# GNN kernel: the words of edge counts are written by ScalarE as 16-bit integers into their place, instead of through a float copy and GpSimd

## The reference

```python
def _ngcf_conv(x, W1, W2, src, dst, n_nodes):
    deg_out = clip(segment_sum(ones, src), 1.0); deg_in = clip(segment_sum(ones, dst), 1.0)
    norm = rsqrt(deg_out[src] * deg_in[dst])
    h_src, h_dst = x[src], x[dst]
    msg = (h_src @ W1 + h_src * h_dst @ W2) * norm[:, None]
    return x @ W1 + segment_sum(msg, dst, n_nodes)

h = maximum(layernorm(x), 0.0)
h = relu(conv(h, W1_1, W2_1)); h = conv(h, W1_2, W2_2)
return x + h
```

## Time and profile before

| | |
|---|---|
| median of the runs | 516.54 us |
| the profiled execution | 518.48 us, its span 516.8 us |
| busy, share of the span | PE 94%, PEld 88%, DVE 79%, ACT 49%, POOL 43% |
| granted TensorE clock, mean | 0.981 |
| chain that ended last | PE 72%, DVE 17%, issue 5%, ACT 2%, DMA 2%, POOL 1% |
| largest groups | `los` L663 136.3 us; `slab` L895 128.2; `hots` L1025 118.7; `words` L463 79.2; `saved` L1034 53.4 |

### The profile page before, as it was taken

The page is one execution under the profiler, slowest core; times in us unless marked ns, Lnnn a source line. Parts: engine busy times, 40 slices in busy tenths (PEclk is TensorE's granted clock), DMA queues, the critical chain, the costliest instruction groups (busy, mean ns, idle before and its releaser), DMA issues.

```text
span 516.8 us, 19829 instructions
## 1 busy us (share of the span) xinstructions
PE 485.1 (94%) x7949; PEld 455.4 (88%) x7949; DVE 410.2 (79%) x1040; ACT 252.4 (49%) x726; POOL 220.9 (43%) x425
## 2 busy tenths in 40 slices
PE   2699999989997997999999999999999999999995
PEld 2577788878786887999999999999999999999995
DVE  6978999999999986987777777776766666666662
ACT  0279999999998795433333333333111121112111
POOL 3336879788999483453333433333100001100000
PEclk9879999999999898999999999999999999999998
DMA  2257102020201000000000000000000110020011
GB/s 68 82 95 94 47 21 64 3 63 3 65 1 43 2 3 1 3 4 2 3 4 3 3 3 2 3 4 3 3 1 3 21 26 1 3 44 1 3 29 20
DMA packets 17912, 10.89 MB, mean 21 GB/s; under 512 B 14144, under 2 KB 16496, under 8 KB 17821
## 3 DMA queue, kind: packets, MB, share of 16 engines
q1 hardware_dynamic: 17117, 7.60, 7.7%
q0 software_dynamic: 672, 2.01, 1.4%
q10 hardware_dynamic: 32, 0.01, 0.0%
HBM read 6.21 MB, written 3.33 MB: 18 GB/s over the span
## 4 chain that ended last, share of the span: by engine, by line
PE 72%; DVE 17%; issue 5%; ACT 2%; DMA 2%; POOL 1%; SPq 0%; DVEq 0%; ACTq 0%; POOLq 0%
PE diff L988 34%; PE iota_bank L988 17%; DVE los L663 9%; PE slab L895 8%; PE diff L879 4%; PE diff L959 2%; PE diff L966 1%; DVE stats L671 1%; ACT hots L1025 1%; PE slab L937 1%; DMA los<-in_dst_dram 1%; PE diff L955 1%; PE turn_t L937 1%; DVE rows L652 1%; DVE late L704 1%
## 5 line engine op out<-in xcount | busy, mean ns | idle before, releaser
L663 DVE TENSOR_TENSOR los<-mixed,iota_bank 128x5120 bf16<-128x5120 bf16 x49 | 136.3, 2810 | 7.0 <-PE slab L895 6.9
L895 PEld LDWEIGHTS slab<-hots,los 128*128 128x128 bf16 x2352 | 122.0, 99 | 17.5 <-issue 4.4
L895 PE MATMUL slab<-hots,los 128*128 128x98 fp8e5 x2352 | 128.2, 211 | 3.0 <-DVE los L663 2.9
L551 POOL TENSOR_TENSOR work<-work,h 128x64 f32<-128x64 f32 x98 | 31.4, 321 | 214.7 <-DVE work L774 214.7
L1025 ACT ACTIVATE hots<-diff 128x784 f16<-128x784 f32 x147 | 118.7, 847 | 9.1 <-PE diff L879 8.8
L988 PE MATMUL diff<-late,mixed 128*128 128x128 f16 x1616 | 104.4, 219 | 0.0
L988 PEld LDWEIGHTS diff<-late,mixed 128*128 128x128 fp8e4 x1616 | 98.7, 99 | 0.4
L988 PE MATMUL diff<-los,mixed 128*128 128x129 f16 x1470 | 95.7, 220 | 0.0
L988 PEld LDWEIGHTS diff<-los,mixed 128*128 128x128 fp8e4 x1470 | 89.3, 98 | 0.3
L463 POOL TENSOR_SCALAR words<-saved 128x784 uint16<-128x784 uint16 x49 | 79.2, 1617 | 7.8 <-ACT saved L1034 7.4
L879 PE MATMUL diff<-select,mixed 80*128 80x392 f16 x294 | 69.4, 342 | 8.4 <-ACT hots L1025 5.0
(11 more groups left out here) (172 smaller groups left out, 537.8 us busy)
## 6 DMA issues: line engine op xcount, KB each, us to landing
x_sb<-in_x_dram SPq DMA_DIRECT2D x4, 384.0 KB
rows_table<-rows SPq DMA_DIRECT2D x6, 252.0 KB
mixed<-rows_table SPq DMA_DIRECT2D x18, 84.0 KB
out_dram<-x_sb SPq DMA_DIRECT2D x8, 128.0 KB
los<-in_dst_dram SPq DMA_DIRECT2D x1, 750.0 KB
out_dram<-x_sb SPq DMA_DIRECT2D x4, 80.0 KB
out_dram<-x_sb SPq DMA_DIRECT2D x4, 48.0 KB
rows_table<-rows SPq DMA_DIRECT2D x1, 180.0 KB
```

The source lines that it names most:

```text
L551: nc.gpsimd.tensor_tensor(out=pair[a][:, 1], in0=s_sum[a], in1=h[:, b], op=ALU.mult).then_inc(product_ready, 1)
L663: nc.vector.tensor_tensor(out=los[:, b % LOS_RING].rearrange("e s (v t) -> e s v t", t=2), in0=key, in1=val, op=ALU.is_equal).then_inc(los ...
L895: ins = nc.tensor.matmul(to, los[:, u // 2 % LOS_RING, u % 2 * ULOWS + low], pairs, start=(step == 0), stop=(step == USTEPS - 1), skip_gro ...
```

## The change

- `words` gets 18 slots (SLOTS) for each block and `v` instead of 16 words: slots 0 to 7 hold the first unit's words, 10 to 17 the second's, 8 and 9 the two units' out-degrees.
- ScalarE's `save_words` writes 16-bit integers into `words` itself: 441 elements, in the order of the PSUM columns, so single elements 36 bytes apart. For even units the groups run downwards (place 8 - group), so that the histogram lies beside the other unit's. There is no `saved` and no MAGIC.
- GpSimd only adds the histograms, both at once as one 32-bit integer for each `v` (49 elements, not 98), `hist` being pairs of 16 bits; L729 takes these apart.
- `unpack` waits for the save instead of the copy, and reads 50 x 2 runs of 4 words of 32 bits.
- A value over 65535 isn't wrapped any more. So VectorE looks for words of 65535: 48 `max` operations over 900 elements each in the second layer, a comparison and a reduction in position 96; the totals' matmul, now of three columns, moves to position 97 after matmul 23, and the comparisons to the end of position 97.

```diff
@@ names
+SLOTS = 18
+FULL = 65535.0
-SAVED_RING = 2
-MAGIC = 2.0 ** 23
-    words = sb("words", [128, BLOCKS, Q, WORDS], U16)
+    words = sb("words", [128, BLOCKS, Q, SLOTS], U16)
-    saved = sb("saved", [128, SAVED_RING, 2, COLS], FP32)
-    hist = sb("hist", [128, 2, Q - 1], I32)
+    hist = sb("hist", [128, Q - 1], I32)
+    largest = sb("largest", [128, Q * SLOTS], U16)
+    hist_of = hist[:].bitcast(U16).rearrange("p (q i) -> p q i", i=2)
+    LARGEST_BESIDE = {BLOCKS + 3: (1, 2), BLOCKS + 4: (3, 4), BLOCKS + 5: (5, 6), **{BLOCKS + b - 1: (b,) for b in range(7, BLOCKS - 2)},
+                      POSITIONS - 3: (BLOCKS - 2, BLOCKS - 1)}
@@ GpSimd
-            def keep_words(b):
+            def add_degrees(b):
                 pool.wait_ge(slab_saved, 2 * b + 2)
-                ...
+                pool.wait_ge(hist_added, b + 1)
+                nc.gpsimd.tensor_tensor(out=hist[:], in0=hist[:],
+                                        in1=words[:, b, 0:Q - 1, WORDS // 2:WORDS // 2 + 2].bitcast(I32)[:, :, 0],
+                                        op=ALU.add).then_inc(hist_added, 1)
@@ VectorE, unpack
-                    dve.wait_ge(words_copied, n + 1)
-                packed = words[:, n % BLOCKS].rearrange("p q w -> p (q w)").bitcast(I32).rearrange(
-                    "p (q w) -> p q w", w=WORDS // 2)
+                    dve.wait_ge(slab_saved, 2 * n + 2)
+                pairs = words[:, n % BLOCKS].rearrange("p q s -> p (q s)").bitcast(I32)
+                packed = bass.AP(pairs.tensor, pairs.offset,
+                                 [pairs.ap[0], [SLOTS // 2, Q], [SLOTS // 2 - WORDS // 4, 2], [1, WORDS // 4]])
@@ VectorE, hand-over
-            nc.vector.tensor_tensor(out=rdo[:], in0=hist[:, 0], in1=hist[:, 1], op=ALU.add).then_inc(deg_summed, 1)
+            nc.vector.tensor_tensor(out=rdo[:], in0=hist_of[:, :, 0], in1=hist_of[:, :, 1], op=ALU.add).then_inc(deg_summed, 1)
@@ VectorE, positions (the check at n == BLOCKS + 4 goes)
+                for b in LARGEST_BESIDE.get(n, ()):
+                    if b > 1:
+                        dve.wait_ge(largest_taken, b - 1)
+                    nc.vector.tensor_tensor(out=largest[:], in0=largest[:] if b > 1 else flat_words[:, 0:Q * SLOTS],
+                                            in1=words[:, b].rearrange("p q s -> p (q s)"),
+                                            op=ALU.max).then_inc(largest_taken, 1)
+                if n == POSITIONS - 2:
+                    dve.wait_ge(largest_taken, BLOCKS - 1)
+                    v(nc.vector.tensor_scalar(largest[:], largest[:], FULL, None, ALU.is_ge))
+                    nc.vector.tensor_reduce(out=totals[:, 2:3], in_=largest[:], axis=AX.X,
+                                            op=ALU.max).then_inc(totals_ready, 1)
+                if n == POSITIONS - 1:
+                    dve.wait_ge(totals_summed, 1)
+                    ...
@@ TensorE, products and the totals
-                    to = bass.AP(mine.tensor, mine.offset, [mine.ap[0], [(group + 1) * BLOCKS, 2], [1, BLOCKS]])
+                    place = (8 - group if u % 2 == 0 else group + 1) * BLOCKS
+                    to = bass.AP(mine.tensor, mine.offset, [mine.ap[0], [place, 2], [1, BLOCKS]])
-                    if n == BLOCKS + 2 and q == LATE:
-                        pe.wait_ge(totals_ready, 1)
+                    if n == POSITIONS - 1 and q == EARLY - 3:
+                        pe.wait_ge(totals_ready, 2)
@@ ScalarE, save_words
-                if u // 2 >= SAVED_RING:
-                    act.wait_ge(words_copied, u // 2 - SAVED_RING + 1)
-                    act.wait_ge(hist_added, u // 2 - SAVED_RING + 2)
-                nc.scalar.activation(saved[:, u // 2 % SAVED_RING, u % 2], slab[u % 2][:, 0:COLS], ACT.Copy,
-                                     bias=MAGIC).then_inc(slab_saved, 1)
+                to = words[:, u // 2, 0:Q - 1, WORDS // 2 + u % 2]
+                to = bass.AP(to.tensor, to.offset, [to.ap[0], [1 if u % 2 else -1, 9], [SLOTS, Q - 1]])
+                nc.scalar.activation(to, slab[u % 2][:, 0:COLS].rearrange("p (s v) -> p s v", v=Q - 1),
+                                     ACT.Copy).then_inc(slab_saved, 1)
```

More of the change, by code:

```diff
@@ L176, in fast_path @@
     rdo_sc0 = sb("rdo_sc0", [128, BLOCKS], FP32)
-    totals = sb("totals", [128, 2], FP32)
-    checks = sb("checks", [1, 2], FP32)
+    totals = sb("totals", [128, 3], FP32)
+    checks = sb("checks", [1, 3], FP32)
     of_stats = stats[:].rearrange("p b s -> p (b s)")
     deg_in, root_in, root, rdi, rdi_rdo, degrees = [of_stats[:, i * BLOCKS:(i + 1) * BLOCKS] for i in range(6)]
-    flat_words = words[:].rearrange("p b q w -> p (b q w)")
+    flat_words = words[:].rearrange("p b q s -> p (b q s)")
     fine = []
     for t in range(TILES):
-        at = t * 4 * SPAN if t < EARLY_TILES else (BLOCKS - 9 + 2 * (t - EARLY_TILES)) * Q * WORDS
+        at = t * 4 * SPAN if t < EARLY_TILES else (BLOCKS - 9 + 2 * (t - EARLY_TILES)) * Q * SLOTS
         home = late if t < EARLY_TILES else flat_words
@@ L196, in fast_path @@
     junk = los_1[0:ROWS, 3 * GROUPS + 2 * WINDOW:3 * GROUPS + 2 * WINDOW + TILES * SAMPLES].rearrange("p (t e) -> p t e", t=TILES)
-    words_late = flat_words[:, (BLOCKS - 3) * Q * WORDS:].bitcast(FP32)
+    words_late = flat_words[:, (BLOCKS - 3) * Q * SLOTS:].bitcast(FP32)
     wabs = words_late[:, 448:512]
@@ L316, in fast_path @@
     totals_summed = sem("totals_summed")
+    largest_taken = sem("largest_taken")
     y_ready = sem("y_ready")
@@ L446, in _ @@
                                     base=0, pattern=[[-1, 128]], channel_multiplier=1).then_inc(consts, 1)
[L447 removed]
+            nc.gpsimd.memset(hist[:], 0).then_inc(hist_added, 1)
             nc.gpsimd.memset(words[:, :, Q - 1:Q, :], 0).then_inc(consts, 1)
@@ L528, in _ @@
             for u in range(UNITS):
-                if u % 2 == 1:
-                    keep_words(u // 2)
+                if u % 2 == 1 and u // 2 < BLOCKS - 1:
+                    add_degrees(u // 2)
                 if u in FETCH_AFTER:
@@ L830, in _ @@
                                             op=ALU.add).then_inc(totals_ready, 1)
[L831 to L834, removed]
                 if n < POSITIONS:
@@ L844, in _ @@
                         unpack(n + 3, (2, 3))
+                for b in LARGEST_BESIDE.get(n, ()):
[11 more added lines that the diff above has]
+                    dve.wait_ge(totals_summed, 1)
+                    v(nc.vector.tensor_scalar(checks[:, 0:2], sum_ps[0:1, 0:2], float(EDGES), None, ALU.is_equal))
+                    v(nc.vector.tensor_scalar(checks[:, 2:3], sum_ps[0:1, 2:3], 0.0, None, ALU.is_equal))
+                    v(nc.vector.tensor_tensor(out=checks[:, 0:1], in0=checks[:, 0:1], in1=checks[:, 1:2], op=ALU.mult))
+                    v(nc.vector.tensor_tensor(out=flag[:], in0=checks[:, 0:1], in1=checks[:, 2:3], op=ALU.mult))
         @block.tensor
@@ L993, in _ @@
                         weigh(weighs[q])
-                    if n == BLOCKS + 2 and q == LATE:
-                        pe.wait_ge(totals_ready, 1)
-                        nc.tensor.matmul(sum_ps[0:1, 0:2], ones[:], totals[:], start=True,
+                    if n == POSITIONS - 1 and q == EARLY - 3:
+                        pe.wait_ge(totals_ready, 2)
+                        nc.tensor.matmul(sum_ps[0:1, 0:3], ones[:], totals[:], start=True,
                                          stop=True).then_inc(totals_summed, 1)
```

3 lines of the change are left out of this document (1 added, 2 removed).

## The result

The kernel after the change takes 643.51 us (median of 4 runs, 643.26 to 643.7), the one before 516.55 in the same session: 1.2445 times as long (interval 1.2414 to 1.2476). I had forecast 540, range 507 to 546. The direction was right, the size was not: +127 us instead of +23.5.

A forecast was written before the change was run, and what follows sets the result against it. TensorE, VectorE and ScalarE nearly full in the first stage, TensorE in the layers. +20.7 + 1.5 - 1.35 + 0.8 + 0.4 + 1.4 = +23.5 on the profiled 518.48 gave 542.0, less 1.94: 540 us, range 507 to 546.

The forecast's parts named there:

- ScalarE's save: First stage, per unit: strided 16-bit write at 1.79 ns per element, 0.40 us more, 0.95 in all.
- my own sum: First stage on ScalarE: 43 blocks of 3.77 us, keys 5.1, table load and root 1.5: 168.7 against 148, +20.7.
- the excess over 3.23: First stage: 43 blocks took 8.9 us over TensorE's 3.23 each, put down to VectorE operations stretched beside GpSimd's.
- The fill rows: VectorE's 49-element fills, strided and dense, both 99 ns; taken as support for a save unchanged at 545 ns.
- a cost above 2.2 ns: Rival, per element of the save: over 0.58 us more each, block over 4.1, kernel 552 us or more; chance 0.08.
- my bounds: Save's time: lower 545 ns, as dense; upper 0.95 us, at the 1.79 ns per element of GpSimd's copy.
- The slower save's way to the end: First stage: ScalarE sets the pace at 3.77 us per block, without idle time; TensorE waits for `hots`.
- GpSimd and the hand-over: Copies gone: blocks -7.4 us if ScalarE isn't late, else nothing; between first stage and layers `rdo` -1.35, longer saves +0.8.
- the rival with a free save: ScalarE writes at a stride as fast as densely: -6.95 us, kernel 509.6; chance 0.37.
- Unpacking: Layers: reading runs of 4 words costs +0.03 us each; rival of one word per cycle, about 533, chance 0.03.
- The search: Second layer: 48 `max` operations at 0.61 us, 0.54 after overlap, mostly in VectorE's idle time; +0.4 us in all.
- The last check: Last position: comparison and reduction over 900 elements make TensorE wait about 1.4 us, +1.4 straight to the end.

The follow-up runs named there:

- run 5: Kernel before with more single reads and writes appended: 441 lone 16-bit reads 36 bytes apart 983 ns, dense 572; 440 elements written in pairs 560.
- run 1: Kernel before with single writes of 441 elements appended, alone: 16-bit 36 bytes apart 2060 ns, 32-bit 951, dense 16-bit 543.
- Run 6: The change, but ScalarE's save writes 441 4-byte floats 36 bytes apart, words wrong, flag set to 1: 537.5 us, 1.0401 of before.
- run 2: The change, but ScalarE's save writes its 441 integers densely, words in wrong order, flag set to 1: 513.22 us, 0.9922 of before.
- run 3: The change with the save's two loops exchanged, writing runs of 9 integers to the same places: 514.19 us, 0.9932 of before.
- run 7: run 3 with the totals' matmul 23 matmuls later in the last position: 511.12 us, 0.9901 of before.

## Why the prediction was wrong

- **ScalarE's save is the step that failed: "I take the upper value", 0.95 us, +0.40 per save.** The mechanism was right, the term was mis-sized: +1.15 on the save and +0.34 on the `hots` behind it, 1.49. With 5.94 us per block in my own sum, and 42 blocks (next point): 42 x 5.94 + 6.6 = 256.1, against 148: +108. The trace has 256.7, from the `los` of block 8 at 61.43 (50.01 before) to the save of block 47's second unit at 318.13 (198.00 before). The other 13.5 of the 122.2 us: blocks 0 to 5 end 11.4 later, where the sum had 1.5, and from that save to the first layer it takes 7.45 instead of 5.35.
- **A block too many.** At 198.0 TensorE was through with block 47, not 48. The save of block 47's second unit starts there, while four slabs, two of each block, run from 195.56 to 200.20:

```profile
195.56 4.64 PE L895 MATMUL slab<-hots,los 128*128 128x98 fp8e5 x96
198.00 0.54 ACT L1034 ACTIVATE saved<-slab 128x441 f32<-128x441 f32 x1 [0.49 <-PE slab L895]
```

So the 148 us hold 42 blocks of 3.52, and the excess over 3.23 is 12.3 us, not 8.9 (43 x 3.23 would also be 138.9, not 139.1). The forecast with 42 blocks is 3.8 lower, 536. It did not decide the outcome.
- **How the size was missed.** I took 1.79 ns per element from GpSimd's copy. That is the price of a lone 16-bit read (run 5), and happens to be that of a lone 32-bit write (run 1). A lone 16-bit write has 4.4, and of before I had no row whose duration holds one. The fill rows looked like one and weren't. The other source, the 2.50 ns of the Trainium skill's Vector Engine (DVE) Microarchitecture Reference, section 5.2, gave 1.3 us as an estimate and fell short of the 2.16 measured as well. I had put 0.08 on a cost above 2.2 ns; both ends of my bounds were durations of something else, and I let them bound the case. What the sum left out is the width of the element: run 1 has 951 ns for 32 bits and 2060 for 16 at the same 36 bytes.
- **The slower save's way to the end** was right: ScalarE without idle time, TensorE waiting for `hots`, 92.8 us. Run 6 confirms the path and, with 42 blocks, the sum: 537.5 for 536. From the `los` of block 8 to `rdo` it takes 165.5 us, 16.5 more than before, where 42 x 3.77 + 6.6 is 16.9 more than 148. Not foreseen was that the cost spills into the next instruction.
- **GpSimd and the hand-over** had the right sign and too large a size. `rdo` got shorter by 1.33 (1.35 forecast), but the hand-over only by 0.5 (5.35 to 4.84 in runs 2, 3 and 7), because the addition behind it then waits 0.84 us for TensorE's last slab (L739 in run 3). The blocks gained 5.3 to 5.8 us (7.4 forecast). So the rival with a free save came out at 513.2 (run 2) instead of 509.6. In the profiled executions the first layer starts 5.9 us earlier in run 3 and 8.5 in run 7 (8.75 forecast). Of the 2.6 between the two, 2.2 are there by the `los` of block 8: from 27.5 to 32.5 us the granted clock was 0.50 (1.2 GHz) in run 3 and in the kernel before, and 1.00 (2.4 GHz) in run 7. So 5.9 is the figure of the change. From there to the end run 3 takes 315.1 us, 1.7 more than before (1.8 forecast).
- **Unpacking** was unchanged in the layers, 350 to 359 ns each. **The search** at 617 ns a piece (0.61 forecast). **The last check** made TensorE wait 1.33 us (1.4 forecast), and moving the matmul takes the wait away, for which the forecast hadn't looked.

## What to carry to other kernels

Before a write is laid out, ask which loop is innermost on the side of SBUF: 16-bit elements must come in pairs that fill a 32-bit word, or in longer runs, and if one side has to be strided, let it be the read. Where nothing in a trace shows the very operation (side, width, distance), the nearest row is not a bound. And a short record isn't a fast operation: look at the idle time before it and at the start of what follows. Before a stretch is divided by a count of blocks, find the row of the last one.

## What the runs showed of the hardware that I had not expected

- Lone 16-bit writes to SBUF: 4.4 ns per 16-byte stretch entered on ScalarE (2060 ns for 441 elements 36 bytes apart; VectorE 2041, GpSimd 2074); lone 32-bit writes 1.74; pairs of 16 bits at 36 bytes have nearly full speed (560 ns for 440).
- Even 49 such elements cost: 380 against 217 ns.
- VectorE's fill of 441 is recorded with 426 ns either way, while strided ones follow each other at 2.01 us and dense ones at 0.59; the missing time stands ahead of the record.
- Matmul outputs at a step of 9 floats in PSUM: 24 in 2.02 us instead of 1.12. ScalarE's reads of PSUM at a step of 49 floats cost nothing (601 against 602 ns).
- With TensorE idle for a third of the time (busy 68.6 of 100 us), its granted clock averaged 0.89 instead of 0.99 to 1.00, that is partly 1.2 instead of 2.4 GHz, and a `slab` matmul took 225 ns instead of 211 on the mean. What that cost was not measured; in the blocks ScalarE was late anyway.
